# Two of four tiles of a state-space and mixture-of-experts kernel transposed by DMA instead of TensorE

## The reference

```python
def _L0_attn_ref(x, ...):
    s = sigmoid(silu(x @ s_w1.T + s_b1) @ s_w2.T + s_b2)
    u = (x @ B_w.T + B_b) * s
    h_t = h_{t-1} @ A.T + u_t            # scan over 4096 steps, state of 128
    y = hs @ C_w.T + C_b + x @ D_w.T + D_b
    return y * sigmoid(x @ g_w.T + g_b)
def _L0_ffn_ref(x, gate_w, expert_w):
    chosen = argmax(x @ gate_w.T)        # one of 8 experts for each row
    return x + expert_w[chosen] @ x      # per row
x = x + _L0_attn_ref(_layernorm(x), ...)
x = x + _L0_ffn_ref(_layernorm(x), ...)
```

## Time and profile before

| | us |
|---|---|
| median of 3 runs | 942.37 (942.27 to 943.14) |
| profiled execution, its own time | 941.93 |
| its span | 940.2 |
| TensorE busy | 916.2 (97%) |
| VectorE busy | 682.9 (73%) |
| ScalarE busy | 618.9 (66%) |
| GpSimd busy | 388.2 (41%) |

### The profile page before, as it was taken

One profiled execution on the slowest core, in us unless ns is written; L12 is line 12 of the kernel. 1 busy time (PEld: TensorE's weight loads), 2 busy tenths in 40 slices (PEclk: granted clock), 3 DMA queues, 4 the chain that ended last, 5 costly groups with the idle time before them and its releaser, 6 DMA issues.

```text
span 940.2 us, 15990 instructions
## 1 busy us (share of the span) xinstructions
PE 916.2 (97%) x4641; PEld 750.2 (80%) x4642; DVE 682.9 (73%) x1670; ACT 618.9 (66%) x874; POOL 388.2 (41%) x508
## 2 busy tenths in 40 slices
PE   7999999999999999999999999999998999999995
PEld 7777888888888888888888888888776788888884
DVE  6686979788797978888797978877875454444442
ACT  5567685867767586776868586776355566666661
POOL 1031537182543618163452717255242453333332
PEclk9999999999999999999999999999999999999998
DMA  8436384847547474765737376565989676555431
GB/s 316 119 90 146 81 203 111 202 119 173 155 115 192 116 209 103 173 151 137 191 90 210 105 191 137 156 162 141 341 306 379 223 259 204 166 160 165 142 115 37
DMA packets 179305, 159.52 MB, mean 170 GB/s; under 512 B 103957, under 2 KB 137493, under 8 KB 178208
## 3 DMA queue, kind: packets, MB, share of 16 engines
q1 hardware_dynamic: 168288, 124.86, 49.8%
q0 software_dynamic: 10800, 33.70, 10.0%
q10 hardware_dynamic: 144, 0.07, 0.0%
HBM read 81.63 MB, written 54.68 MB: 145 GB/s over the span
## 4 chain that ended last, share of the span: by engine, by line
PE 91%; DVE 2%; ACT 1%; issue 1%; POOL 0%; ACTq 0%; POOLq 0%
PE y L1539 21%; PE y L1272 7%; PE y L1274 7%; PE y L1273 7%; PE gates L1272 7%; PE gates L1274 6%; PE gates L1273 6%; PE scan L1405 3%; PE turned L1446 3%; PE gates L1446 3%; PE scan L1272 2%; PE scan L1274 2%; PE scan L1273 2%; PE scores L1528 2%; PE turned L1528 2%; PE scores L1362 2%
## 5 line engine op out<-in xcount | busy, mean ns | idle before, releaser
L1539 PE MATMUL y<-experts,x1T_hi 128*128 x568 | 183.9, 405 | 2.8 <-issue 1.5
L539 POOL TENSOR_SCALAR ln_var_eps<-ln_mean_var 128x4 f32<-128x4 f32 x16 | 3.6, 224 | 304.1 <-DVE ln_mean_var L947 304.0
L586 POOL DMA_INDIRECT out<-gate,ids x71 | 70.3, 990 | 138.9 <-DVE gate L1247 97.7
L1539 PEld LDWEIGHTS y<-experts,x1T_hi 128*128 128x128 f32 x568 | 102.5, 190 | 22.9 <-issue 4.2
L1247 DVE TENSOR_TENSOR gate<-y,raw_weights 128x512 f32<-128x512 f32 x71 | 49.1, 691 | 93.3 <-PE y L1539 93.1
L1539 PE MATMUL y<-experts,x1T_lo 128*128 x284 | 112.3, 395 | 0.0
L1272 PE MATMUL gates<-GwT_hi,xT_hi 128*128 128x512 f32 x256 | 104.8, 410 | 0.0
L1272 PE MATMUL y<-DwT_hi,xT_hi 128*128 128x512 f32 x256 | 102.0, 399 | 0.5 <-DVE gateT L869 0.5
L694 ACT ACTIVATE joined<-flipped 128x1024 uint16<-128x1024 uint16 x60 | 82.3, 1372 | 30.0 <-DVE xT_lo L1090 26.2
L1274 PE MATMUL y<-DwT_hi,xT_lo 128*128 128x512 f32 x256 | 100.7, 393 | 0.0
L1273 PE MATMUL y<-DwT_lo,xT_hi 128*128 128x512 f32 x256 | 100.6, 393 | 0.0
(11 more groups left out here) (270 smaller groups left out, 2324.1 us busy)
## 6 DMA issues: line engine op xcount, KB each, us to landing
raw_weights<-routed_rows SPq DMA_DIRECT2D x71, 258.0 KB, 2.7
x_in<-L_attn_x SPq DMA_DIRECT2D x32, 512.0 KB, 4.8
x_rows<-L_attn_x SPq DMA_DIRECT2D x32, 512.0 KB, 4.7
turned_experts<-raw_weights SPq DMA_DIRECT2D x32, 512.0 KB, 4.8
experts<-turned_experts SPq DMA_DIRECT2D x8, 2048.0 KB, 11.4
raw_weights<-L_ffn_expert_w SPq DMA_DIRECT2D x32, 256.0 KB, 3.0
routed_rows<-padrow SPq DMA_DIRECT2D x9, 258.0 KB
out<-gate,ids POOLq DMA_INDIRECT x71, 2.9
```

Source lines behind the costliest of these rows:

```text
L586: nc.gpsimd.indirect_dma_start(out=out_rows, out_offset=bass.IndirectOffsetOnAxis(ap=ids[r][:, 0:1], axis=0), in_=res[r], in_offset=None, ...
L1539: ins = nc.tensor.matmul(Y[m % 2][:], x2T[a][:, k, m % 2 * P:(m % 2 + 1) * P], flat[:, bass.ds(first + (w * KD + k) * D, D)], start=(k == ...
```

## The change

For blocks b = 0 to 13 (whose tail runs in blocks 1 to 14), tiles 2 and 3 of x1 are no longer turned by TensorE. ScalarE copies each into two 16-bit planes (`halve_x1`) in rows 0 and 1 of y_biased, SyncE issues a DMA transpose into rows 2 and 3, ScalarE joins the planes back into rows 0 and 1 (`join_x1`), and tail_hi and tail_lo read from there. In TensorE's list the eight products of pair 0 stay where they were, four and four, without transposes between them. On ScalarE the plane copies come ahead of the next block's halves, the joins and tail_hi of tiles 2 and 3 behind scoresT of pair 0, and join(2) of the next block behind the state copies. On VectorE tile 2's lo part moves behind over(2) and tile 3's behind over(3). On SyncE the two transposes go ahead of the flips of the next block. Blocks 14 and 15 have the old order.

```diff
+        def by_dma(b, i):
+            return b < LASTB - 1 and i >= NT // 2
+        x1_halves = [yb[:, j, :].bitcast(u16) for j in range(2)]
+        x1_flipped = [yb[:, 2 + j, :].bitcast(u16).rearrange("p (c t) -> p c t", t=P) for j in range(2)]
+        x1_joined = [yb[:, j, :] for j in range(2)]
@@ sync, in a block
+                if b > 0 and not last:
+                    for j in range(2):
+                        sp.wait_ge(S_["x1_halves"], 2 * (b - 1) + j + 1)
+                        sp.dma_start_transpose(x1_flipped[j], x1_halves[j]).then_inc(x1_turned[j], 16)
                 for n in range(NB):
                     if not last:
                         flip(b + 1, 2 * n)
@@ scalar
             def tail_hi(b, i):
-                act.wait_ge(S_["x2T_psum"], NT * b + i + 1)
+                if by_dma(b, i):
+                    act.wait_ge(S_["x1_joined"], 2 * b + i - 1)
+                    src = x1_joined[i - 2].rearrange("p (k t) -> p k t", k=KD)
+                else:
+                    act.wait_ge(S_["x2T_psum"], on_pe(b, i))
+                    src = by_block(turn_bank(b, i))
+            def halve_x1(b, i):
+                act.wait_ge(S_["x1_ready"], NT * b + i + 1)
+                nc.scalar.activation(x1_halves[i - 2].rearrange("p (h d) -> p h d", h=2), planes(xrow[b % 2][:, i, 0:D]), ACT.Copy
+                                     ).then_inc(S_["x1_halves"], 1)
+            def join_x1(b, i):
+                act.wait_ge(x1_turned[i - 2], 16 * (b + 1))
+                nc.scalar.activation(planes(x1_joined[i - 2]), x1_flipped[i - 2].rearrange("p (h k) t -> p h (k t)", h=2), ACT.Copy
+                                     ).then_inc(S_["x1_joined"], 1)
@@ scalar, body
+                if tail and ahead:
+                    halve_x1(b - 1, 2)
+                    halve_x1(b - 1, 3)
                 if ahead:
                     halve(b + 1, 0)
                     halve(b + 1, 1)
                 else:
                     join_piece(b, 0)
                     join_piece(b, 1)
-                if tail:
                     tail_hi(b - 1, 2)
                     tail_hi(b - 1, 3)
+                if tail:
                     scoresT(b - 1, 0)
-                    if ahead:
-                        join_piece(b, 0)
+                if tail and ahead:
+                    for i in range(2, NT):
+                        join_x1(b - 1, i)
+                        tail_hi(b - 1, i)
+                    join_piece(b, 0)
...
-                    join(b + 1, 2)
+                    if not tail:
+                        join(b + 1, 2)
...
                 if ahead:
+                    if tail:
+                        join(b + 1, 2)
                     high(b + 1, 2)
@@ vector, body
                 over(b, 0)
-                if tail:
+                if not ahead:
                     tail_lo(old, 2)
...
                 over(b, 2)
-                if tail:
+                if tail and ahead:
+                    tail_lo(old, 2)
+                elif tail:
                     tail_lo(old, 3)
                 over(b, 3)
+                if tail and ahead:
+                    tail_lo(old, 3)
                 gate_sum(b, 1)
@@ tensor, body
                 to_chunks(b)
-                if tail:
+                if b == LASTB:
                     tail_turn(b - 1, 1 - q, 2, True)
+                elif tail:
+                    for n in range(KD):
+                        score_product(b - 1, 0, n)
                 gates(b, 0, 1, 2)
                 over(b, 0)
-                if tail:
+                if b == LASTB:
                     tail_turn(b - 1, 1 - q, 3, True)
+                elif tail:
+                    for n in range(KD, 2 * KD):
+                        score_product(b - 1, 0, n)
                 gates(b, 0, 3)
```

More of the change, by code:

```diff
@@ L191, in preln_ssm_moe_kernel @@
                      "rank_psum pos_ready picked_ready run_ready dest_ready ids_ready ends_ready pad_sent "
-                     "experts_in table_step slot_iota_made expert_table need_table row_table "
+                     "x1_halves x1_joined experts_in table_step slot_iota_made expert_table need_table row_table "
                      "slot_norm slot_turned slot_hi slot_lo slot_psum slot_base slot_ids slot_result").split():
@@ L199, in preln_ssm_moe_kernel @@
         x_turned = [sem("x_turned_even"), sem("x_turned_odd")]
+        x1_turned = [sem("x1_turned_third"), sem("x1_turned_fourth")]
         xres_loaded = [sem("xres_loaded_even"), sem("xres_loaded_odd")]
@@ L307, in turn_bank, with on_pe @@
             return ((SA, G) if b == LASTB else (TP, Y[NT - 1]))[i % 2]
+        def by_dma(b, i):
+            return b < LASTB - 1 and i >= NT // 2
+        def on_pe(b, i):
+            return NT // 2 * min(b, LASTB - 1) + NT * max(0, b - LASTB + 1) + i + 1
+        x1_halves = [yb[:, j, :].bitcast(u16) for j in range(2)]
+        x1_flipped = [yb[:, 2 + j, :].bitcast(u16).rearrange("p (c t) -> p c t", t=P) for j in range(2)]
+        x1_joined = [yb[:, j, :] for j in range(2)]
         def score_bank(b):
@@ L640, in tail_hi @@
             def tail_hi(b, i):
-                act.wait_ge(S_["x2T_psum"], NT * b + i + 1)
-                nc.scalar.activation(turned_rows(b, i)[0][:, :, i % 2 * P:(i % 2 + 1) * P], by_block(turn_bank(b, i)), ACT.Copy
-                                     ).then_inc(S_["x2T_hi"], 1)
+                if by_dma(b, i):
[4 more added lines that the diff above has]
+                    src = by_block(turn_bank(b, i))
+                nc.scalar.activation(turned_rows(b, i)[0][:, :, i % 2 * P:(i % 2 + 1) * P], src, ACT.Copy
+                                     ).then_inc(S_["x2T_hi"], 1)
+            def halve_x1(b, i):
[6 more added lines that the diff above has]
+                                     ).then_inc(S_["x1_joined"], 1)
             def scoresT(b, pair):
@@ L952, in tail_lo @@
                 hi, lo = [h[:, :, i % 2 * P:(i % 2 + 1) * P] for h in turned_rows(b, i)]
-                nc.vector.tensor_tensor(lo, by_block(turn_bank(b, i)), hi.bitcast(f32), ALU.subtract
+                src = x1_joined[i - 2].rearrange("p (k t) -> p k t", k=KD) if by_dma(b, i) else by_block(turn_bank(b, i))
+                nc.vector.tensor_tensor(lo, src, hi.bitcast(f32), ALU.subtract
                                         ).then_inc(S_["x2T_lo"], 1)
@@ L1322, in y_dense @@
                     if i == NT - 1:
-                        wait(pe, S_["x2T_lo"], NT * b)
+                        wait(pe, S_["x2T_lo"], NT * b if b == LASTB else NT * (b - 1) + 2)
                 dense(Y[i], i, DwT, ks, False)
```

## The result

| | before | after |
|---|---|---|
| median, us | 942.75 (942.27 to 943.38, 4 runs) | 962.86 (960.67 to 964.40, 4 runs) |
| profiled execution, us | 941.93 | 961.89 |
| its span, us | 940.2 | 960.1 |

The changed kernel takes 1.0223 times as long (95% interval 1.0201 to 1.0246), 20.1 us more. The forecast was 959, with a range of 948 to 976.

What follows compares the result with a forecast made beforehand. TensorE, 91% of the chain of waits, was taken to bound the kernel. A block gains 0.89 us, but two waits leave TensorE 1.20 us late: 14 x 1.20 = 16.8 us more, 959 us, range 948 to 976.

Steps and rivals of the forecast that it cites:

- The gain of the transposes: TensorE, between score products of tiles 0 and 1: eight transposes fewer save 0.89 us a block, 12.5 us in all.
- The first wait: TensorE's late score products wait 1.4 us a block for VectorE's low half of tile 3, leaving TensorE 0.54 us late.
- SBUF instead of PSUM: VectorE's low-half subtraction, now reading SBUF, was taken at 0.68 us; at 1.56 the first wait would be 0.88 longer.
- The second wait: TensorE's turning back of scores waits 0.66 us for ScalarE's second scoresT, starting at 303.14; TensorE is then 1.20 us late.
- Sum: Over the whole kernel: 14 blocks at 1.20 us make 16.8 us more, so 959 us.
- The queues: SyncE's new DMA transposes, landing after 4.2 us in the median, and the later flips were taken to cost nothing.
- D: Rival: new DMA transposes land late, at 6.3 us, adding 1.1 us a block to the second wait; 974 us; 10%.
- joins waiting for DMA: Sign of a wrong forecast: ScalarE's joins standing idle for DMA transposes; no size given.
- E: Rival: TensorE's waits lower its clock, costing 1.1 to 1.65 us a block; 974 to 982 if every block fell; 13%.
- B: Rival: only VectorE's wait counts, as ScalarE gains 0.66 us somewhere; 14 x 0.54 = 7.6 us, 950 us; 12%.
- C: Rival: faster, tile 3's low half is ready when TensorE comes and both waits vanish; 930 us; 3%.
- F: Rival: transposes were free between score products, nothing is won, both waits start earlier; some 2.1 us a block, 971 us; 5%.

Runs made afterwards that it cites:

- the two pairs of runs: TensorE's transposes put back, result unread, against the changed kernel with VectorE's and ScalarE's orders changed: 948.06 against 937.34 us; with the gate sum first: 942.50 against 929.31 us.
- experiment 1: Changed kernel with only VectorE's order changed, tile 2's low half after over(1), tile 3's after over(2): 977.79 us, ratio to before 1.0353.
- experiment 2: Changed kernel with only ScalarE's order changed, the second scoresT right behind the first rounding of the next block: 948.61 us, ratio to before 1.0068.
- experiment 7: Changed kernel with the store of the second expert piece issued behind the first two flips of the next block: 957.85 us, ratio to before 1.0165.
- experiment 3: Changed kernel with both VectorE's order (low halves earlier) and ScalarE's order (second scoresT earlier) changed: 937.34 us, ratio to before 0.9941.
- experiment 5: As experiment 3, with tile 2's low half on VectorE moved behind the gate sum: 929.31 us, ratio to before 0.9865.

## Why the prediction was right, step by step

- **The gain of the transposes**, 0.445 us a tile: 0.91 - 0.48 and 0.92 - 0.46 in the records; by the periods 0.90 and 0.87 us a block in the two pairs of runs, for 0.89. Right.
- **The first wait.** The low half starts at 305.69 - 6.19 = 299.50 (299.55 forecast) and takes 0.69 (0.68). The products start 0.39 us later than before, not 0.54: from VectorE's end to the matmul it was 0.05 us, not 0.16. The weight load here is of 16 columns, the one of the earlier trace rows of 128; that this makes the difference fits the rows, but no experiment separates it. A size off by 0.15 us, without effect on the sum, as the second wait takes it up.
- **SBUF instead of PSUM** for the subtraction: 0.69 and 0.70 us in all rows shown; the 1.56 of the earlier trace rows did not come.
- **The second wait.** scoresT at 303.14 for 303.14; 0.67 us for 0.66. Experiments 1 and 2 show that it alone decides: without the first the period stays (42.74 for 42.76 where the clock holds), without the second it falls to 42.06, and the time by 14 us (10 by the period, the rest with the late blocks).
- **Sum.** 1.14 us a block for 1.20, 16.0 for 16.8. That the median then lies 4 us above the forecast comes from the next two terms. The waits in the records were named as 18 and 8 us and were 16.1 and 11.2.
- **The queues**, cost at nothing, were the term set too low. The new transposes landed after 3.3 us in the median and 6.1 at most, in time in all blocks but the first, where a join waited 0.43 us for one; so D, 1.1 us in every block, did not come. But the flips behind them landed after up to 10.0 us instead of 6.3, which I had called free because their joins are 2.6 us later. In block 12 that did not suffice. It was a sign of being wrong that I had named, joins waiting for DMA, and it applied in these two blocks. Every kernel here with the new transposes has flips that land after 9.0 to 10.0 us, so they go with them; by which way was not settled (experiment 7 excludes the store ahead of them). Such blocks make up what lies between 959 and 962.86, as far as the profiled execution shows it.
- **The clock** (E). Stands of 1.15 and 0.67 us, one after the other, left it at 1.00; one of 1.80 brought it down, and those of about 1.5 us and more in experiment 1 did in 11 of 14 blocks. It is not the length alone: in experiment 1 stands of 1.48 and 1.49 us were followed by a fall and three of 1.51 and 1.52 were not, and in experiment 3 one of 1.83 was not. The forecast took an example from the Trainium skill, "TensorE: Matmul & The Clock Gate", section "HAM oscillation — how this bites in real kernels", a loop throttled in every turn. There TensorE waits some 3 to 5 us for DMA in each turn, so the example did not reach the waits forecast here, and "all 14 blocks" did not follow from it. Experiment 1 shows nearly the same with shorter stands, the changed kernel does not.
- **B, C, F** as forecasts of this kernel are refuted by the same rows. B's price (950) is what experiment 2 measured, C's (930) what experiment 5 measured. The forecast was right by its mechanism in 12 of the 14 blocks, and the range had room for the other two.

## What to carry to other kernels

Work taken off the engine that is never idle pays only if nothing that this engine waits for moves later by more than the slack it had; find for each consumer on it the producer's place in its own list, before and after. Where two waits stand one behind the other and the later one's producer does not wait for the first, only the later one counts, and taking away the first alone can make things worse. An engine with idle time in sum can still be late: put the short instruction that another engine waits for ahead of the long ones that have time.

## What the runs showed of the hardware

A fall of TensorE's clock to half (1.2 GHz) came after stands as short as about 1.5 us in experiment 1; the stretch from 187.0 to 190.4 us, at 0.55, lies behind one of 1.48. Stands of the same length and up to 1.83 us also passed without one. A DMA transpose of 128 x 1024 two-byte elements (the flips of x) landed 3.0 us after its issue at best, and 6.3 us at most in the kernel before and 10.0 in the changed one. Four TensorE transposes of 128 x 128 float32 between score products cost 0.43 to 0.45 us by the periods of the blocks (0.38 to 0.47 by the medians), measured by putting them back.
